# The last two blocks of a fused attention and expert layer: head 0's additions on VectorE alone, the experts' results added a block earlier, the final projection per head and scaled when added

## The reference

```python
xn = _layernorm(x)
q, k, v = xn @ Wq, xn @ Wk, xn @ Wv                     # 16 heads of 64
attn = softmax(q @ k.T * 64 ** -0.5)
a = (attn @ v).reshape(s, 1024) @ Wo + bo
e = argmax(softmax(xn @ router_w.T))                    # one expert of 8 for each token
f = square(relu(xn @ expert_fc[e])) @ expert_proj[e]
return x + a + f
```

## Time and profile before

| | |
|---|---|
| median of three runs | 1435.21 us (1434.1 to 1436.35) |
| the profiled execution | 1433.47 us, its span 1431.7 us |
| granted TensorE clock, mean of the span | 0.989 |
| busy: PE | 1394.3 us, 97% |
| busy: PEld | 859.2 us, 60% |
| busy: DVE | 1163.4 us, 81% |
| busy: ACT | 736.6 us, 51% |
| busy: POOL | 1083.7 us, 76% |
| POOL additions (L437, `acc` and `ex`) | 668, mean 1333 ns |
| DVE additions (L702) | 228, mean 1262 ns |
| block 31, from its first scores to the last product with V | about 1379 to 1421 us |
| from there to the end | about 1421 to 1431.7 us |

### The profile page before, as it was taken

One profiled execution on the slowest core, in us unless ns is written; L12 is line 12 of the kernel. 1 busy time (PEld: TensorE's weight loads), 2 busy tenths in 40 slices (PEclk: granted clock), 3 DMA queues, 4 the chain that ended last, 5 costly groups with the idle time before them and its releaser, 6 DMA issues.

```text
span 1431.7 us, 20036 instructions
## 1 busy us (share of the span) xinstructions
PE 1394.3 (97%) x6427; PEld 859.2 (60%) x6427; DVE 1163.4 (81%) x1543; ACT 736.6 (51%) x1314; POOL 1083.7 (76%) x858
## 2 busy tenths in 40 slices
PE   5899999999999999999999999999999999999996
PEld 3555666566656666656656666666665665656553
DVE  7889978888788788878788778887778788878865
ACT  4254555555545545555545554555555554545552
POOL 8279777767777767777777777777777777789996
PEclk8899999999999999999999999999999999999998
DMA  3423111321122211221113211133102231000000
GB/s 81 109 57 91 41 41 25 89 66 41 41 53 61 65 42 41 72 66 41 41 41 91 63 38 28 43 89 88 41 3 61 64 70 23 23 16 21 10 23 15
DMA packets 64967, 72.09 MB, mean 50 GB/s; under 512 B 8928, under 2 KB 38112, under 8 KB 64864
## 3 DMA queue, kind: packets, MB, share of 16 engines
q1 hardware_dynamic: 63840, 68.72, 19.4%
q0 software_dynamic: 1024, 2.10, 0.5%
HBM read 17.83 MB, written 5.11 MB: 16 GB/s over the span
## 4 chain that ended last, share of the span: by engine, by line
PE 87%; DVE 7%; issue 2%; POOL 2%; ACT 1%; SPq 1%; DMA 0%; POOLq 0%; DVEq 0%
PE OB L1024 28%; PE SB L996 16%; PE MB L1012 15%; PE SB L1000 14%; DVE mx L686 3%; PE XB L1061 2%; PE XB L1052 2%; PE XB L1070 2%; POOL acc L437 2%; PE XB L986 1%; PE XB L979 1%; DVE acc L702 1%; PE XB L1031 1%; PE XB L1033 1%; PE XB L1032 1%
## 5 line engine op out<-in xcount | busy, mean ns | idle before, releaser
L437 POOL TENSOR_TENSOR acc<-acc,ex 128x512 f32<-128x512 f32 x668 | 876.7, 1333 | 155.3 <-ACT ex L536 128.0
L536 ACT ACTIVATE ex<-SB 128x512 f32<-128x512 f32 x1024 | 608.1, 598 | 471.5 <-PE SB L1000 414.2
L686 DVE TENSOR_REDUCE mx<-MB 128x1 f32<-128x512 f32 x1024 | 683.4, 687 | 187.6 <-PE MB L1012 185.3
L1024 PE MATMUL OB<-ex,V 128*64 128x512 f32 x2048 | 466.1, 597 | 0.0
L996 PE MATMUL SB<-Q,K 128*128 128x512 f32 x1024 | 426.9, 417 | 0.0
L1012 PE MATMUL MB<-K,Q 128*128 128x512 f32 x1024 | 405.6, 400 | 7.0 <-DVE mx L686 6.2
L1000 PE MATMUL SB<-Q,K 128*128 128x512 f32 x1024 | 401.2, 392 | 1.6 <-DMA Q<-mrow 1.6
L702 DVE TENSOR_TENSOR acc<-acc,ex 128x512 f32<-128x512 f32 x228 | 287.8, 1262 | 30.2 <-POOL acc L437 19.7
L1024 PEld LDWEIGHTS OB<-ex,V 128*64 128x64 f32 x2048 | 138.4, 137 | 270.2 <-issue 238.2
L996 PEld LDWEIGHTS SB<-Q,K 128*128 128x128 f32 x1024 | 193.7, 189 | 139.0 <-issue 103.0
L1012 PEld LDWEIGHTS MB<-K,Q 128*128 128x128 f32 x1024 | 193.8, 190 | 58.8 <-DVE mx L686 16.5
(11 more groups left out here) (125 smaller groups left out, 567.3 us busy)
## 6 DMA issues: line engine op xcount, KB each, us to landing
Q<-qhi SPq DMA_DIRECT2D x124, 128.0 KB, 2.8
K<-khi SPq DMA_DIRECT2D x112, 128.0 KB, 2.3
Q<-qlo SPq DMA_DIRECT2D x64, 128.0 KB, 2.6
K<-klo SPq DMA_DIRECT2D x56, 128.0 KB, 2.3
w<-fc SPq DMA_DIRECT2D x23, 256.0 KB, 2.8
w<-projT SPq DMA_DIRECT2D x23, 256.0 KB, 3.6
sorted_x<-res SPq DMA_DIRECT2D x1, 1472.0 KB, 7.0
tok<-sorted_x SPq DMA_DIRECT2D x23, 64.0 KB, 1.8
```

Of the source, the lines that this page charges most:

```text
L437: pool.tensor_tensor(a[:, :], src[:, :], EX[h][ex_slot(kt)][:, :], ALU.add).then_inc(done, 1)
L536: act.activation(EX[h][ex_slot(kt)][:, :], SB[in_ring(2 * kt + h)][:, :], ACT.Exp).then_inc(a_e[h], 1)
L686: dve.tensor_reduce(mx[:, m % 2, u:u + 1], MB[in_ring(i)][:, :], AX.X, ALU.max).then_inc(v_m, 1)
L1024: mm = pe.matmul(OB[own[h], :], V[(n // JB) % 2][:, k, own[h]], EX[h][ex_slot(k)][:, :], start=(k == 0), stop=(k == NT - 1))
```

## The change

It has four parts.

1. `on_pool` gives no addition of head 0 to POOL in block 31 and none from kt 9 on in block 30. In block 31 DVE makes the addition of every kt in that kt, and the group of the block's end in `last` is gone. The group of block 30's end, at kt 0 of block 31, stays and has three additions instead of one.
2. `FETCH` now is kt 2, 4, 6, 8, 11, 14 in blocks 28 and 29 and kt 1, 3, 5, 7 in block 30.
3. `take_back` moves from block 31 (kt 1, 2, 3, 5) to block 30 (kt 12 to 15).
4. The tail is rebuilt. PE makes the denominators by eight matmuls with `acc` as weights and one column of ones, so that they come out with queries on partitions, 128x8 in all. DVE takes one reciprocal of these 128x8. `osb` is not scaled: PE multiplies each head's half of it with the half of Wo (eight matmuls over 64 rows), and DVE's scalar_tensor_tensor multiplies the result with the reciprocal as a scalar per partition and adds it to `Y`, once per quarter and head, eight in all.

The diff, with blank lines and the declaration of a semaphore left out (the first `last` is DVE's, the second PE's):

```diff
-FETCH = [(n, kt) for n in (NB - 4, NB - 3) for kt in (2, 5, 8, 11, 14)] + [(NB - 2, kt) for kt in range(2, 13, 2)]
-BACK = (1, 2, 3, 5)
+FETCH = [(n, kt) for n in (NB - 4, NB - 3) for kt in (2, 4, 6, 8, 11, 14)] + [(NB - 2, kt) for kt in range(1, 8, 2)]
+BACK = (12, 13, 14, 15)
...
         def on_pool(n, kt):
+            if n.off == NB - 1 or (n.off == NB - 2 and kt >= 9):
+                return False
             return kt % BATCH == 1 or (kt % BATCH == 2 and n.off != 1)
...
-        LAST = [SB[0], SB[1], MB[0], MB[1]]
+        LAST = [SB[0:2], MB[0:2]]
...
-                        if kt % BATCH == 0:
+                        if n.off == NB - 1:
+                            if kt == 0:
+                                add_own(n, kt)
+                            else:
+                                add(n, kt)
+                        elif kt % BATCH == 0:
                             add_own(n, kt)
-                        if n.off == NB - 1 and kt in BACK:
+                        if n.off == NB - 2 and kt in BACK:
                             take_back(BACK.index(kt))
...
                 def last():
-                    def invert_tile(q):
-                        dve.reciprocal(rd[:, cols(q)], XB[:, cols(q)]).then_inc(v_rd, 1)
-                    def normalise_tile(q):
-                        dve.wait_ge(v_rd, 2 * (NB - 1) + q + 1)
-                        dve.wait_ge(a_o, NB)
-                        dve.tensor_tensor(on[:, cols(q)], osb[:, cols(q)], rd[:, cols(q)], ALU.mult).then_inc(v_on, 1)
-                    def sum_tile(q):
+                    def sum_head(q, h):
                         y = Y[:, NT - TB + q, :]
-                        dve.wait_ge(v_back, JB)
-                        dve.wait_ge(t_wo, NB + q)
-                        dve.tensor_tensor(y, LAST[q][:, 0:P], y, ALU.add).then_inc(v_y, 1)
-                    for t in range(NT - BATCH + 1, NT):
-                        if not on_pool(Lin(NB - 1), t):
-                            add(Lin(NB - 1), t)
+                        if h == 0:
+                            dve.wait_ge(v_back, JB)
+                            dve.wait_ge(t_wo, NB + q // 2)
+                        else:
+                            dve.wait_ge(v_y0, q + 1)
+                        dve.scalar_tensor_tensor(out=y, in0=LAST[q // 2][h][:, q * P:(q + 1) * P], scalar=rd[:, 2 * q + h:2 * q + h + 1],
+                                                 in1=y, op0=ALU.mult, op1=ALU.add).then_inc((v_y0, v_y)[h], 1)
                     dve.wait_ge(t_den, NB)
-                    for q in range(TB + 2):
-                        if q < TB:
-                            invert_tile(q)
-                        if 1 <= q < TB + 1:
-                            normalise_tile(q - 1)
-                        if q >= 2:
-                            sum_tile(q - 2)
+                    dve.reciprocal(rd[:, 0:2 * TB], XB[:, 0:2 * TB]).then_inc(v_rd, 1)
+                    dve.wait_ge(v_rd, 2 * (NB - 1) + 1)
+                    sum_head(0, 0)
+                    for q in range(TB):
+                        if q + 1 < TB:
+                            sum_head(q + 1, 0)
+                        sum_head(q, 1)
...
                 def last():
                     times_v(Lin(NB - 1), NT - 1, 1)
-                    denominators(Lin(NB - 1))
+                    n = Lin(NB - 1)
+                    take_spare(v_rd, 2 * (NB - 1) + 1)
+                    for h in range(2):
+                        wait(pe, sums[h][n % 2], added(n, NT - 1))
+                    for q in range(TB):
+                        for h in range(2):
+                            mm = pe.matmul(XB[:, 2 * q + h:2 * q + h + 1], acc[h][n % 2][:, q * P:(q + 1) * P], ones[:, 0:1],
+                                           start=True, stop=True)
+                    mm.then_inc(t_den, 1)
+                    pe.wait_ge(a_o, NB)
                     pe.wait_ge(v_m, UNITS * NB)
                     for q in range(TB):
-                        pe.wait_ge(v_on, q + 1)
-                        pe.matmul(LAST[q][:, 0:P], on[:, q * P:(q + 1) * P], wo_s[(PAIRS - 1) % 2][:, :],
-                                  start=True, stop=True).then_inc(t_wo, 1)
+                        for h in range(2):
+                            mm = pe.matmul(LAST[q // 2][h][:, q * P:(q + 1) * P], osb[own[h], q * P:(q + 1) * P],
+                                           wo_s[(PAIRS - 1) % 2][own[h], :], start=True, stop=True)
+                        if q % 2:
+                            mm.then_inc(t_wo, 1)
```

More of the change, by code:

```diff
@@ L201, in layer @@
         d_q0 = sem("d_q0_")
-        v_on = sem("v_on")
+        v_y0 = sem("v_y0")
         d_out = sem("d_out")
@@ L903, in last @@
                 def last():
-                    def cols(q):
-                        return slice(q * P, (q + 1) * P)
-                    def invert_tile(q):
-                        dve.reciprocal(rd[:, cols(q)], XB[:, cols(q)]).then_inc(v_rd, 1)
-                    def normalise_tile(q):
-                        dve.wait_ge(v_rd, 2 * (NB - 1) + q + 1)
-                        dve.wait_ge(a_o, NB)
-                        dve.tensor_tensor(on[:, cols(q)], osb[:, cols(q)], rd[:, cols(q)], ALU.mult).then_inc(v_on, 1)
-                    def sum_tile(q):
-                        y = Y[:, NT - TB + q, :]
-                        dve.wait_ge(v_back, JB)
-                        dve.wait_ge(t_wo, NB + q)
-                        dve.tensor_tensor(y, LAST[q][:, 0:P], y, ALU.add).then_inc(v_y, 1)
-                    for t in range(NT - BATCH + 1, NT):
-                        if not on_pool(Lin(NB - 1), t):
-                            add(Lin(NB - 1), t)
-                    dve.wait_ge(t_den, NB)
-                    for q in range(TB + 2):
-                        if q < TB:
-                            invert_tile(q)
-                        if 1 <= q < TB + 1:
-                            normalise_tile(q - 1)
-                        if q >= 2:
-                            sum_tile(q - 2)
+                    def sum_head(q, h):
+                        y = Y[:, NT - TB + q, :]
+                        if h == 0:
[5 more added lines that the diff above has]
+                                                 in1=y, op0=ALU.mult, op1=ALU.add).then_inc((v_y0, v_y)[h], 1)
+                    dve.wait_ge(t_den, NB)
+                    dve.reciprocal(rd[:, 0:2 * TB], XB[:, 0:2 * TB]).then_inc(v_rd, 1)
[5 more added lines that the diff above has]
+                        sum_head(q, 1)
                 schedule(dve, first, one, last)
```

## The result

The changed kernel takes 1425.89 us (median of four runs, 1425.02 to 1426.37) against 1434.74 us (1434.1 to 1436.35): a ratio of 0.9935 with a 95% interval of 0.9921 to 0.9949, 8.85 us less. The forecast was 7.4 us less, to 1427.8, with a range from 1425.6 to 1431.9: the direction held, and the time lies at the range's lower end. Its profiled execution took 1426.19 us, 7.28 less than the one of before, so by the two traces the forecast of 7.4 looks exact. That was luck: the price of the fetches was 1.6 us too low and the gain at the stop 1.6 us too low, and the two cancel. The gap between 7.28 and 8.85 has a cause of its own.

The account below looks back on a forecast made before the run. Bounds: POOL's backlog stopping PE through DVE in block 31, and the end after the last addition. Additions -5.6, fetches +0.1 and tail -1.9 sum to -7.4, giving 1426.1 profiled and 1427.8 us median; 8-in-10 range 1425.6 to 1431.9.

Parts of the forecast that it names:

- V end to last addition: End of block 31, from PE's last product with V to POOL's last addition: -1.3 us, within part 1's 5.6.
- The bounds of the kernel: Block 31: POOL's backlog stops PE for 4.57 us through DVE's additions and reciprocal; second bound is the end.
- Part 2, the fetches: Blocks 28 to 30: one more fetch ahead of `normalise` falls mostly into POOL's idle time; +0.1 us.
- the bound of 0.9: Blocks 28 to 30: upper bound in us on the fetches' cost; a rival at 0.1 had this and more.
- the projection's margin: Block 29: 0.2 to 0.4 us between `normalise` and PE's projection, its weight load a little before.
- Part 1, prices and stop: Block 31: DVE additions at 1.79 pitch, stop shrinks from 4.7 to 1.8 us, last addition 5.6 us earlier.
- The rival's price, a pitch of 2.0: DVE's long chains: additions never overlap POOL's, last addition 3 us later, 1430.8 us; chance 0.15.
- The cover of the moved `take_back`s: Block 30: DVE's free time after the maxima hides them at no cost; without it 4 x 1.7 = 6.8 us.
- The clock: Behind block 31's stop: 1.8 us idle keeps full clock, so projection with kt 12 costs 1.84, not 3.30.
- The rival in which a short stop lowers the clock: Block 31 to the end: the 1.8 us stop halves the clock and it stays so, 1440.8 us; chance 0.04.
- The tail: After the last addition: new denominators, projections and DVE operations end T + 7.4 against T + 9.4; -1.9 us taken.
- The anchor: Final step: the median lies 1.74 us above the profiled execution, turning 1426.1 into 1427.8.

Follow-up runs that it names:

- e3: The kernel before with only the new division of additions (old fetch list, old place of the experts' results, old tail): 1428.74 us, ratio 0.9959.
- e7: The changed kernel with fetches at kt 2, 5, 8, 10, 12, 14 in blocks 28 and 29 and 2, 4, 6, 8 in block 30: 1424.28 us.
- e5: The changed kernel with the experts' results added in block 31 again (kt 1, 2, 3, 5): 1429.74 us, ratio 0.9967.
- e6: The changed kernel with block 30's additions of head 0 from kt 9 on left with POOL as before: 1425.64 us, ratio 0.9938.
- e1: The kernel before with only the new fetch list: 1433.96 us against 1434.73, ratio 0.999.
- e8: The changed kernel with POOL's additions of block 31 cut to one column (work left out): 1424.76 us in one execution.

## Why the prediction was right or wrong, point by point

Counted as above, and with the forecast's own steps:

| step | forecast | traces |
|---|---|---|
| fetches, blocks 28 to 30 | +0.1 | +1.67 (p30 less the 0.13 of p27) |
| the stop ahead of the projection | -2.9 | -4.49 (p30 to p31: 37.07, now 32.58) |
| clock behind the stop | -1.46 | -1.40 (p31 to V end: 13.61, now 12.21; -2.70 by the second trace of before) |
| V end to last addition | -1.3 | -1.50 (+1.38, now -0.12) |
| last addition to end | -2.0, 0.1 taken back | -2.18 (9.33, now 7.15) |
| drift before block 28 | none | +0.13 |
| sum | -7.4 (the second to fourth row stood in it as 5.6) | -7.77 |

**The bounds of the kernel: right.** POOL's backlog reached PE through DVE's additions and reciprocals. E3 takes away the backlog and 2.3 of the 4.6 us, and the end follows.

**Part 2, the fetches: wrong**, by the step "the new one falls behind kt 4, where POOL idled 0.89, so 0.1 to 0.3 is left", and with it the bound of 0.9. I counted what the fetch does to POOL's own queue. The damage is done elsewhere. DVE in block 28, kt 7 and 8, before and then after:

```profile
1285.48 2.36 DVE L702 TENSOR_TENSOR acc<-acc,ex 128x512 f32<-128x512 f32 x2
1287.77 1.74 DVE L833 RECIPROCAL rd<-rd 128x256 f32<-128x256 f32 x1
1289.43 3.60 DVE L686 TENSOR_REDUCE mx<-MB 128x1 f32<-128x512 f32 x6
```

```profile
1286.16 3.86 DVE L705 TENSOR_TENSOR acc<-acc,ex 128x512 f32<-128x512 f32 x2
1289.94 1.74 DVE L836 RECIPROCAL rd<-rd 128x256 f32<-128x256 f32 x1
1291.61 3.60 DVE L689 TENSOR_REDUCE mx<-MB 128x1 f32<-128x512 f32 x6
```

With POOL's queue shifted, both of DVE's additions now meet one of POOL's (3.86 us for two, where one slipped through and two took 2.36). The reciprocal and the maxima behind them are 1.5 us late for it (3.86 less 2.36). The waits of the changed kernel in that stretch, which have no counterpart before:

```profile
PEld MB L1010 <- DVE mx L689: 1.4, 1, 1.4
PE MB L1010 <- DVE mx L689: 0.9, 1, 0.9
POOL osb L446 <- DVE rd L836: 0.9, 1, 0.9
```

From here to projection 31 PE waits for DVE's maxima twice, 0.9 us in block 28 and 0.5 in block 30, and for nothing else; before, it does not wait at all. PE stands for DVE's maxima, and POOL stands idle for the reciprocal where I had feared its queue would be too full. I had named the projection's margin as the risk; the maxima I had not looked at.

**Part 1, prices and stop: the mechanism right, two sizes wrong.** DVE's additions of kt 5 to 8 in block 31 of the changed kernel; the first and the second row end a group, the third and fourth are the single pieces of the x3:

```profile
1395.98 0.69 DVE L705 TENSOR_TENSOR acc<-acc,ex 128x512 f32<-128x512 f32 x1 [1.07 <-ACT ex L539]
1396.95 4.79 DVE L705 TENSOR_TENSOR acc<-acc,ex 128x512 f32<-128x512 f32 x3 [0.28 <-ACT ex L539]
1401.67 1.74 DVE L836 RECIPROCAL rd<-rd 128x256 f32<-128x256 f32 x1
...
1398.48 1.59 DVE L705 TENSOR_TENSOR acc<-acc,ex 128x512 f32<-128x512 f32 x1
...
1400.17 1.58 DVE L705 TENSOR_TENSOR acc<-acc,ex 128x512 f32<-128x512 f32 x1
```

Four additions and the way to the reciprocal take 1401.67 - 1395.98 = 5.69 us, and I had 6.9. The pitch of the chain, from the start of one addition to the start of the next, is 1400.17 - 1398.48 = 1.69, not 1.79: the 1.79 of rows 3 runs from the first of a group, which started 0.15 us after one of POOL's (at 1391.90) and had nearly the whole of it to wait for; within the chain it is 0.51 (1398.48 against 1397.97). And the first addition of each group is not slowed (0.69), since head 0's exponential comes half a step before head 1's and POOL has not begun. Twice 1.2 us is 2.4, of which DVE gave back 1.07 waiting for kt 5; so the stop went from my 1.8 to nothing in the changed kernel and to 0.3 in e7, where PE is not late. The rival's price, a pitch of 2.0, is refuted: 1.69 for one of DVE and one of POOL, where the lone durations 0.69 and 1.27 add up to 1.96. Its mechanism is not. POOL's additions beside the two single ones of DVE:

```profile
1397.97 1.55 POOL L440 TENSOR_TENSOR acc<-acc,ex 128x512 f32<-128x512 f32 x1
1399.66 1.54 POOL L440 TENSOR_TENSOR acc<-acc,ex 128x512 f32<-128x512 f32 x1
```

They end at 1399.52 and 1401.20, and DVE's at 1400.07 and 1401.75. So DVE's ends 0.55 us after POOL's, and POOL's next 1.13 after DVE's: each needs 0.14 us less than alone behind the other's end, and 1.96 - 2 x 0.14 = 1.68. That fits strict turns in which the first 0.14 us of an addition may overlap the other's; no run tests it apart. The Trainium skill, SBUF — State Buffer, section Who interferes with whom, calls the ports that the two share an exclusive lock. The trace agrees with that, and not with a price made of the two whole durations.

**The cover of the moved `take_back`s: right.** They cost nothing in block 30, where they take 4.69 us together and PE has no wait between projections 30 and 31, and 2.5 us in block 31 (e5). That block 30's additions had to move as well was assumed and not argued; e6 shows that they need not.

**The clock: the term was right, the reason for it wrong.** I took 1.8 us of idle as no loss from a window of 1.5 us of idle with a clock of 1.00. That window ends with the idle time, and the fall shows behind it: e1 has 1.00 in its stop and 0.50 behind. E3 and e5 lost under 0.1 us after 2.3, e1 lost 1.6 after 2.25. The changed kernel has no stop, so the term came right for a reason that was not in the forecast. The rival in which a short stop lowers the clock has e1 for its first half; in no trace did the low clock then last through to the tail, as it needs for its 1440.8.

**The tail: right in sum.** The one-column denominators took 1.85 us to the next group (1417.41 to 1419.26), forecast 1.8 to 1.9. The projections were faster than I took them: 16 records in 1.16 us (1419.26 to 1420.42) against 1.85. But DVE's eight operations, 0.26 apart against a forecast of 0.24, run on from the first half's product at 1420.13 to 1422.29, so they and not PE's second half set the end. From T to `Y` it is 5.02 us, forecast 5.1.

**The anchor: wrong,** and this is the step that put the time 1.9 us too high. The sum gave 1426.1 for a profiled execution, which took 1426.19. Then I added 1.74, the distance of the old median from its profiled execution, as a constant. In the changed kernel the median lies 0.30 below. The distance was partly the clock behind the stop, which in the profiled execution of before was back early and in a second trace cost 1.3 us more. That is a cost that the change removes, so it had to be in the sum and not in the anchor.

The mean granted clock of every execution supports this. Of 31 executions of the kernel before that were made beside e1 to e8, the four at 0.986 took 1436.5 to 1436.9 us and the seven at 0.989 took 1433.4 to 1434.3. So the spread goes with the clock, as both sources do that the traces show, the start (up to 2.6 us between executions) and the clock behind the stop. How much each has in the gap from 7.28 to 8.85 is open, since a mean over the span does not say where the clock was low.

## What to carry to other kernels

When an instruction is moved on an engine that contends with a second one, look at what the second one's next instructions meet afterwards and who waits behind them, not only at the idle time that the moved one fills. A delay ahead of a stop set by another engine is free, and the same delay costs in full once the stop is gone, so the parts that were measured alone (+0.03 for the fetches, -5.2 for the additions, -1.2 for the tail; the moved results never were) don't add up to the whole (-7.8). Where a stop lowers the clock, take its price from several executions before taking it as a constant, and read it in the windows behind the stop, not in those of the stop.

## What the runs showed of the hardware

- Two 128x512 fp32 additions with both operands in SBUF, one chain on VectorE and one on GpSimd, go at 1.69 us for one of each in chains of four. Alone they take 0.69 and 1.27. In the chain VectorE's ends 0.55 us after GpSimd's, and GpSimd's 1.13 after VectorE's.
- The clock after 4.6 us of idle PE was at 0.50 for 2.8 or for 5.7 us, in two executions of the same kernel, which cost 1.4 or 2.7 us in the 12 us behind. After 2.3 us of idle it stayed at 1.00 in e3 and e5; after 2.25 in e1 it fell to 0.50 and cost 1.6.
- The granted clock while PE stood still was 1.00 in e1 although it fell right behind.
- A 128x128 fp32 weight with one column costs as much as with eight: 16 records in 1.85 us against 8 in 0.9. Projections over 64 rows in pairs, the heads on different halves of the rows, took 1.16 us for 16 records at full clock; over 128 rows 16 would have taken 1.85 by my estimate from the 1.05 of eight in rows 6 and 0.8 for eight more.
